# One of nine harmonics taken out of the product on TensorE, and harmonics loaded in longer runs

## The reference

```python
def tensor_product(x_e, sh, w, C):            # C: [64, 9, 128]
    acc = sh[:, 0:1] * (x_e @ C[:, 0, :])
    for s in range(1, S):                     # S = 9 harmonics
        acc = acc + sh[:, s:s + 1] * (x_e @ C[:, s, :])
    return acc * w
q = (tfn_features @ Wq).reshape(n, H, DQK)
k = tensor_product(x_dst, edge_sh, wk, Cqk).reshape(-1, H, DQK)
v = tensor_product(x_dst, edge_sh, wv, Cv).reshape(-1, H, DV)
attn = jnp.einsum('ehd,ehd->eh', q[edge_src], k)
...                                           # softmax over the edges of a node, sum of v * alpha,
out = tfn_features @ W_self + upd             # W_out, then a batch norm
```

## Time and profile before

| | |
|---|---|
| median of 3 runs | 3127.47 us (3126.22 to 3128.46) |
| profiled execution, span from first to last instruction | 3126.1 us |
| what lies around the span (median less span) | 1.4 us |
| busy over the whole span | PE 79%, PEld 68%, DVE 71%, ACT 28%, POOL 65% |

### The profile page before, as it was taken

The page is one execution under the profiler, slowest core; times in us unless marked ns, Lnnn a source line. Parts: engine busy times, 40 slices in busy tenths (PEclk is TensorE's granted clock), DMA queues, the critical chain, the costliest instruction groups (busy, mean ns, idle before and its releaser), DMA issues. The chain is left out here.

```text
span 3126.1 us, 51454 instructions
## 1 busy us (share of the span) xinstructions
PE 2476.7 (79%) x14006; PEld 2130.6 (68%) x14006; DVE 2209.2 (71%) x5060; ACT 864.2 (28%) x2414; POOL 2032.3 (65%) x2119
## 2 busy tenths in 40 slices
PE   5778787525667667477777767999999999999986
PEld 4777787424666666355555556888888888888862
DVE  4555555526888887555555563888888888888875
ACT  1111111136666663111111110222232222323231
POOL 4777777457777771277777736777776677677710
PEclk9776667657888888599999978999999999999985
DMA  3443333133333330155555557889888898888820
GB/s 84 94 89 86 86 87 86 30 68 64 61 60 60 60 52 4 46 155 160 152 160 152 160 147 179 214 206 214 212 206 205 203 216 206 207 204 205 213 68 11
DMA packets 333760, 404.38 MB, mean 129 GB/s; under 512 B 171136, under 2 KB 203006, under 8 KB 333570
## 3 DMA queue, kind: packets, MB, share of 16 engines
q1 hardware_dynamic: 252034, 251.20, 34.4%
q0 software_dynamic: 66560, 96.41, 14.5%
q10 hardware_dynamic: 14976, 54.53, 5.1%
HBM read 339.81 MB, written 62.07 MB: 129 GB/s over the span
## 5 line engine op out<-in xcount | busy, mean ns | idle before, releaser
L1934 PE MATMUL psum<-ckv,z 128*128 128x256 f32 x4160 | 967.8, 383 | 0.0
L1934 PEld LDWEIGHTS psum<-ckv,z 128*128 128x128 f32 x4160 | 766.7, 191 | 97.9
L1768 POOL DMA_INDIRECT acc<-QW,dst_i x416 | 399.5, 960 | 184.6 <-issue 111.2
L234 POOL DMA_INDIRECT ga<-TA,src_i x416 | 412.4, 991 | 161.6 <-issue 126.5
L1789 POOL DMA_INDIRECT ga<-XX,src_i x416 | 399.5, 960 | 162.8 <-issue 122.5
L1027 POOL DMA_INDIRECT ga<-T,src_i x416 | 401.9, 966 | 151.5 <-issue 125.9
L234 POOL DMA_INDIRECT ga<-T,src_i x416 | 396.6, 953 | 149.3 <-issue 124.7
L2048 DVE TENSOR_TENSOR z<-psum,shb 128x2560 f32<-128x2560 f32 x104 | 293.2, 2820 | 66.7 <-PE psum L1925 66.5
L1121 PE MATMUL psum<-HT,wy 128*128 128x128 f32 x1664 | 264.7, 324 | 70.0 <-DVE wy L1394 69.2
L445 PE MATMUL psum<-wre,re 128*128 128x68 f32 x832 | 215.2, 351 | 119.4 <-DVE oneT L290 67.7
L1121 PEld LDWEIGHTS psum<-HT,wy 128*128 128x128 f32 x1664 | 242.8, 232 | 87.8 <-DVE wy L1394 81.5
(11 more groups left out here) (362 smaller groups left out, 4142.9 us busy)
## 6 DMA issues: line engine op xcount, KB each, us to landing
shb<-in_ea SPq DMA_DIRECT2D x104, 640.0 KB, 6.2
WKV<-wkvo ACTq DMA_DIRECT2D x104, 512.0 KB
shb<-in_ea SPq DMA_DIRECT2D x104, 512.0 KB, 8.5
wkv<-WKV SPq DMA_DIRECT2D x104, 512.0 KB
dl<-DL SPq DMA_DIRECT2D x208, 128.0 KB
win<-TB SPq DMA_DIRECT2D x416, 32.0 KB
ga<-T,src_i POOLq DMA_INDIRECT x832
ef<-in_ea SPq DMA_DIRECT2D x104, 128.0 KB
```

Source lines behind the costliest of these rows:

```text
L234: pool.indirect_dma_start(o, None, table, bass.IndirectOffsetOnAxis(ap=src_i[:, g * GT + t:g * GT + t + 1], axis=0)).then_inc(s_g[k], 16)
L1768: pool.indirect_dma_start(qg[:, (g % QR) * GT + t, :], None, QW, bass.IndirectOffsetOnAxis(ap=dst_i[:, g * GT + t:g * GT + t + 1], axis=0) ...
L1934: last = pe.matmul(kv_of(k)[:, t, :], z[:, k % 2, j, t * 128:(t + 1) * 128], ckv[:, j, :], start=(j == 0), stop=(j == NZ - 1))
```

## The change

The ninth harmonic leaves the product on PE. Its keys and values without the harmonic, `h @ C[:, 8, :]`, are computed once per node (`node_last_harmonic`), copied by DVE to SBUF and written as 256 more columns of `XX`, whose rows are now 384 columns (1536 bytes) instead of 128 (512 bytes). After the gather ACT multiplies those 256 columns of each edge by its ninth harmonic, a scale per partition, and writes the result into PSUM (`last_harmonic`); PE adds the remaining four chunks onto it without clearing it. `seen` runs four matmuls into those banks ahead of the stage. DVE's `z` has four chunks (2048 elements). The ring of gathered rows has three groups instead of four. The host lays out the harmonics so that each partition's run in a load is 8 KB, and the ninth as a column per tile. The node queries are moved behind the new node products. `h` is written to `XX` from `H` by two transfers a half, in 256-byte pieces, and ACT's copy into `twice` is gone.

```diff
-        NZ = 5
+        NZ = 4
+        TR3 = 2 * D + 2 * F
-        XX = dram("XX", [N, 2 * D])
+        XX = dram("XX", [N, TR3])
-        GR = 4
+        GR = 3
...
                     if g >= GR:
                         pool.wait_ge(e3_X, g - GR + 1)
+                        pool.wait_ge(e3_seed, g - GR + 1)
...
-                    sp.dma_start(shb[0:D, k % 2], A["ea9"][0:NS:2, cols].partition_broadcast(D)).then_inc(e3_e[k % 2], 16)
-                    sp.dma_start(shb[D:128, k % 2, 0:NZ - 1], A["ea9"][1:NS:2, cols].partition_broadcast(D)).then_inc(e3_e[k % 2], 16)
+                    sp.dma_start(shb[0:D, k % 2].rearrange("p z e -> p (z e)"),
+                                 A["sh_even"][g:g + 1, :].partition_broadcast(D)).then_inc(e3_e[k % 2], 16)
+                    sp.dma_start(shb[D:128, k % 2].rearrange("p z e -> p (z e)"),
+                                 A["sh_odd"][g:g + 1, :].partition_broadcast(D)).then_inc(e3_e[k % 2], 16)
...
-                    sp.wait_ge(n3_x, h + 1)
-                    sp.dma_start(XX.rearrange("(p j) f -> p j f", p=PN)[:, J, :], twice[:, J].rearrange("p j a f -> p j (a f)")).then_inc(n3_ox, 16)
+                    sp.wait_ge(n3_h, h + 1)
+                    for a in range(2):
+                        sp.dma_start(XX.rearrange("(p j) f -> p j f", p=PN)[:, J, a * D:a * D + D], H[:, J, :]).then_inc(n3_ox, 16)
+                for part in PARTS:
+                    sp.wait_ge(n3_bc, pairs(part[1]))
+                    sp.dma_start(XX.rearrange("(p j) f -> p j f", p=PN)[:, J_of(part), 2 * D:TR3], parts_of[:, J_of(part), :]).then_inc(n3_ox, 16)
...
+                def last_harmonic(i, k):
+                    g = i * UG + k
+                    act.wait_ge(e3_g[k], i * 64 + 64)
+                    wait(act, e3_ev, (g - 1) * 2)
+                    for t in range(GT):
+                        last = act.activation(kv_of(k)[:, t, :], ga[:, (i * UG + k) % GR * GT + t, 2 * D:TR3], ACT.Copy,
+                                              scale=sh_last[:, bass.ds(g * GT + t, 1)])
+                    last.then_inc(e3_seed, 1)
...
                 def products(i, k, t):
                     g = i * UG + k
                     if t == 0:
                         pe.wait_ge(e3_z, g + 1)
-                        wait(pe, e3_ev, (g - 1) * 2)
+                        pe.wait_ge(e3_seed, g + 1)
                     for j in range(NZ):
                         last = pe.matmul(kv_of(k)[:, t, :], z[:, k % 2, j, t * 128:(t + 1) * 128], ckv[:, j, :],
-                                         start=(j == 0), stop=(j == NZ - 1))
+                                         start=False, stop=(j == NZ - 1), skip_group_check=True)
...
+                def node_last_harmonic(r):
+                    j0, n = R3[r]
+                    pe.wait_ge(n3_tc, r + 1)
+                    if r >= 2:
+                        pe.wait_ge(n3_bc, pairs(r - 1))
+                    for j in range(n):
+                        last = pe.matmul(bank[4 + r % 2 * 2 + j // 2][0:PN, j % 2 * 256:j % 2 * 256 + 256],
+                                         HT[:, (j0 + j) * PN:(j0 + j + 1) * PN], c_last[:], start=True, stop=True)
+                        if j % 2 or j == n - 1:
+                            last.then_inc(n3_b, 1)
...
+                for r, (j0, n) in enumerate(R3):
+                    for half, (a, m) in enumerate(rounds(n, 2)):
+                        dve.wait_ge(n3_b, pairs(r) + half + 1)
+                        dve.tensor_copy(parts_of[:, j0 + a:j0 + a + m, :],
+                                        bank[4 + r % 2 * 2 + half][0:PN, 0:m * 256].rearrange("p (j f) -> p j f", j=m)).then_inc(n3_bc, 1)
```

More of the change, by code:

```diff
@@ L1708, in build @@
         NODE3 = len(R3) * 5 + 2
+        pairs = lambda r: sum(len(rounds(n, 2)) for _, n in R3[:r])
+        NOX = 2 * len(HALVES) + len(PARTS)
         e3_zero = sem("e3_zero")
@@ L1720, in build @@
         SPARE = 8
-        ga = tmp("ga3", [128, GR * GT, F])
-        one = tmp("one3", [128, OR * GT, 128])
+        rows3 = tmp("rows3", [128, GR * GT * TR3 + OR * GT * 128])
+        ga = rows3[:, 0:GR * GT * TR3].rearrange("p (t f) -> p t f", f=TR3)
+        one = rows3[:, GR * GT * TR3:GR * GT * TR3 + OR * GT * 128].rearrange("p (t n) -> p t n", n=128)
+        parts_of = rows3[0:PN, 0:NJ * 2 * F].rearrange("p (j f) -> p j f", j=NJ)
         wkv = tmp("wkv", [128, 2, GT, 2 * F])
@@ L1896, in _ @@
                     act.activation(HT[0:D, j0 * PN:(j0 + n) * PN], bank[r % 2][0:D, 0:n * PN], ACT.Copy).then_inc(n3_tc, 1)
-                    if r:
-                        query_rows(r - 1)
-                query_rows(len(R3) - 1)
+                for r in range(len(R3)):
+                    query_rows(r)
                 act.wait_ge(e3_i, 3)
+                act.wait_ge(n3_ox, NOX * 16)
+                act.wait_ge(n3_l, NL3 * 16)
+                act.wait_ge(n3_seen, 4)
                 each_step(act, body)
@@ L1924, in transposes @@
                     for t in range(GT):
[L1925 removed]
+                        last = pe.transpose(bank[0][:, t * 128:(t + 1) * 128], ga[:, (i * UG + k) % GR * GT + t, 0:2 * D], ident[:])
                     last.then_inc(e3_X, 1)
@@ L1970, in node_transposes, with seen @@
                     for j in range(n):
-                        last = pe.transpose(bank[r % 2][0:D, j * PN:(j + 1) * PN], twice[:, j0 + j, 0, :], ident[0:PN, 0:PN])
+                        last = pe.transpose(bank[r % 2][0:D, j * PN:(j + 1) * PN], H[:, j0 + j, :], ident[0:PN, 0:PN])
                     last.then_inc(n3_t, 1)
+                def node_last_harmonic(r):
[8 more added lines that the diff above has]
+                            last.then_inc(n3_b, 1)
+                def seen():
+                    for b in range(2, 6):
+                        pe.matmul(bank[b][:], ident[:], ckv[:, 0:2, :].rearrange("p a f -> p (a f)"), start=True, stop=True)\
+                          .then_inc(n3_seen, 1)
                 def node_queries(r):
@@ L1994, in _ @@
                     if r:
-                        node_queries(r - 1)
-                node_queries(len(R3) - 1)
+                        node_last_harmonic(r - 1)
+                node_last_harmonic(len(R3) - 1)
+                for r in range(len(R3)):
+                    node_queries(r)
                 pe.wait_ge(n3_qc, len(R3))
-                pe.wait_ge(n3_p, 4)
+                pe.wait_ge(n3_bc, pairs(len(R3)))
+                pe.wait_ge(n3_p, 3)
+                seen()
                 pe.sem_inc(e3_S, SPARE)
@@ L2030, in _ @@
                 for J, _ in HALVES:
-                    dve.scalar_tensor_tensor(twice[:, J, 0, :], XC[:, J, :], 0.0, st[:, 5, J].unsqueeze(2).to_broadcast([PN, J.stop - J.start, D]),
+                    dve.scalar_tensor_tensor(H[:, J, :], XC[:, J, :], 0.0, st[:, 5, J].unsqueeze(2).to_broadcast([PN, J.stop - J.start, D]),
                                              ALU.max, ALU.mult).then_inc(n3_h, 1)
@@ L2251 @@
     a["ea64"] = np.pad(a.pop("edge_attr_64"), ((0, fill), (0, 0))).T
-    a["ea9"] = np.pad(a.pop("edge_attr_9"), ((0, fill), (0, 0))).T
+    ea9 = np.pad(a.pop("edge_attr_9"), ((0, fill), (0, 0)))
+    a["sh_last"] = ea9[:, 8].reshape(NT, W).T
+    ea9 = ea9.reshape(NT // GT, GT * W, 9).transpose(0, 2, 1)
+    a["sh_even"] = ea9[:, 0:8:2].reshape(NT // GT, -1)
+    a["sh_odd"] = ea9[:, 1:8:2].reshape(NT // GT, -1)
     a["L2_gnn_WT"] = a.pop("L2_gnn_W").T
```

31 lines of the change are left out of this document (15 added, 16 removed).

## The result

The changed kernel takes 3166.20 us (median of 4 runs, 3143.56 to 3186.18) against 3127.22 before: ratio 1.012, 95% interval 1.0089 to 1.015. It is 1.2% slower, where 3100 was forecast. Its four runs lie 43 us apart, those of the kernel before 2 us. The profiled execution took 3162.97 us with a span of 3161.2, 35.1 more than before.

A forecast was written before the change was run, and what follows sets the result against it. PE was taken as the bound at 10.76 us a group; 10.1 after the change gives -67 us in the stage, +42 ahead, -2 at the end: -27, so 3100 us, range 3072 to 3131.

The forecast's parts named there:

- What bounds the kernel before: Fourth edge stage: PE is the bound at 10.76 us a group, with DVE 0.3 and POOL 0.8 us behind.
- PE's gain, DVE's, z: Per group: PE loses 8 of 40 instructions, 1.86 us, leaving 8.9; DVE's z shrinks by 0.56 us, leaving DVE 9.9.
- ACT's four instructions "at nothing": Scaling after the gather: 1.4 to 2.9 us of ACT a group, costed at nothing; without cover up to 0.7 a group.
- The ring "nothing": Gathered rows in the stage: three groups instead of four leave 17 us of slack, so no cost.
- The harmonics at the old rate: Harmonics loads in the stage: 8 KB runs bring nothing, the rate stays, q1 takes 6.8 us a group.
- The inventory of the DMA: Stage, all 16 engines per group: q1 6.8 us, XX gathers 2.6 to 3.1, QW 1.0, sum 10.4 to 10.9.
- With 1.07 as full, 9.7 to 10.2 us: Stage: dividing the DMA work by a full share of 1.07 gives 9.7 to 10.2 us a group, as near binding as DVE.
- POOL's 10.0 us: Stage: eight gathers a group at 0.95 us work plus 0.30 between make 10.0 us, POOL becoming the bound.
- rival 4: Stage gathers: POOL's issue grows with the row; each 0.1 us costs 42 us, at 0.15 3163 us; chance 0.07.
- The shift ahead of the stage: Table writes before the first gather: longer writes start the stage 42 us later, bounds 24 and 46.
- Rival 2: XX writes from H: 256-byte writes cost far more than loads; at three times 22 ns, 3155 us; chance 0.13.
- Rival 1: Stage: DMA by bytes, softmax steps or ACT's queue hold a group at 10.35 us; 3126, no change; chance 0.16.

The follow-up runs named there:

- before_light: The kernel before, with its harmonics loads bringing only five of the nine harmonics from the third group on: 3127.94 us, ratio 0.9998.
- no_seed: The changed kernel without ACT's four scalings a group, so the ninth harmonic is missing from the sums, all gathered as before: 3168.58 us, ratio 1.0134.
- light_loads: The changed kernel with the harmonics loads bringing only 4 KB of each partition's 8 KB from the third group on: 3111.52 us, ratio 0.9947.
- ring4: The changed kernel with the ring of gathered rows back at four groups: 3166.26 us, ratio 1.0121.
- before_long_runs: The kernel before with only the change's DRAM layout of the harmonics, one run of 10 or 8 KB into each partition: 3127.85 us, ratio 0.9999.
- two_queues: The changed kernel with the odd harmonics' loads issued by ACT two groups ahead, the even ones still by SP: 3208.00 us, ratio 1.0247.
- light_values: light_loads with DVE's product of values and weights cut to one column in sixteen from the third group on: 3088.59 us, ratio 0.9872.
- single_h: The changed kernel with rows of 320 columns (h once), eight PE products by the identity replacing four transposes, and a four-group ring: 3115.74 us, ratio 0.9969.
- distinct_source: The changed kernel with each partition's 8 KB of harmonics loaded from a DRAM row of its own: 3141.82 us, ratio 1.0061.

## Why the prediction was wrong

The order of its steps:

- **What bounds the kernel before** was right: PE, shown by before_light.
- **PE's gain, DVE's, z** were right in size: 32 instructions of products a group, z 2.287 us for 2.27 forecast. PE's clock stayed near full (0.96).
- **ACT's four instructions "at nothing"** was right: no_seed gains nothing. In no_seed the DMA still holds the stage, so it alone would not show this; but in light_loads, where the DMA does not, PE never waits for ScalarE either. They took 4 x 0.463 = 1.9 us, inside 1.4 to 2.9.
- **The ring "nothing"** was right in the sum (ring4). The sign I had named for being wrong, GpSimd waiting on its shorter ring, did appear (44.7 us), but as an effect of late rows.
- **The harmonics at the old rate** was right within the 5% that before_long_runs found. Alone they load at 216 GB/s (212 before). Distinct rows in DRAM leave q1 as it was. The half of the ports that the Trainium skill gives (SBUF — State Buffer, "Door 1: the DMA port swizzle") is neither refuted nor shown; two_queues shows that issuing the loads of both halves at once gains nothing.
- **The inventory of the DMA** was right: 6.69 us for q1 (6.8 forecast) and 3.79 for both gathers (3.6 to 4.1), 10.5 in all (10.4 to 10.9).
- **"With 1.07 as full, 9.7 to 10.2 us" is the step that failed.** I took the share of 9 us in which one kind of load ran with nothing else as the capacity of a stage in which two kinds of gathers and three of loads mix and each load waits for its buffer. In the changed kernel the same 9 us read 1.00 (first row below), and the six kernels that are held by the DMA show 0.97 to 1.01 over 900 us; why a mixed stretch ends there is not shown. 10.5 / 0.97 is 10.8 us, and the rest of the chain followed: PE, VectorE and GpSimd each wait in turn for rows that are late. Of the miss in the stage, 101 x 0.76 = 77 us, light_loads gives 101 x (10.86 - 10.37) = 49 to it.
- **POOL's 10.0 us was mis-sized too**: it is 10.37, the other 0.27 us of the miss against the 10.1 I took, 27 us in all. A gather's price was read as 0.95 us at the stage's start and 0.96 in the steady part; where GpSimd itself is the bound the mean is 0.98 to 1.00, since products of two SBUF tiles hold gathers up. One such product costs 0.21 us a group (light_values against light_loads). The row's length costs nothing (rival 4 falls). The kernel before paid less of this because fewer of its gathers met such a product: between 2000 and 2900 us 29 of 678 were held, against 105 of 695 in light_loads. That it was GpSimd's waiting for VectorE which kept them apart is argued, not shown.
- **The shift ahead of the stage** was +26 to +31, not +42, within the bounds of 24 and 46. Packets of 256 bytes took 0.399 x 12 x 16 / 4256 = 18 ns, of 1,024 bytes 0.34 x 20 x 16 / 2370 = 46 ns, where 22 and 50 were forecast; and shares of 0.40 and 0.34 are 6.4 and 5.4 engines, not five. Rival 2, dear writes below 512 bytes, falls: 18 ns is no more than loads of that size cost (20.4 ns at 221 bytes), so nothing of the read-modify-write for which I had cited the Trainium skill (DMA: Bandwidth & Descriptors, "Specifications") shows in the price. By the byte they are still 1.6 times as dear as the packets of 1,024.

The harmonics' loads alone, 1850 to 1859 us, and the queue's rows for the two stretches of writes, 1864 to 1876 and 1883 to 1903 us:

```profile
1850.00:1859.00 9.00, 2.85 (x10) 2.48 (x10) 8.28 (x25) 1.25 (x3) 0.00 (x0) 0.50 1.00 216
...
q1 hardware_dynamic: 4256, 1.09, 39.9%
...
q1 hardware_dynamic: 2370, 2.42, 34.0%
```

Put right, the sum is 101 x (10.86 - 10.76) + 26 - 1 = +35 us. The sum would have been near it with the same inventory and 0.97: 10.8 us a group, +4 in the stage. Rival 1 named the mechanism (DMA by bytes) but stopped at 10.35 us; with DMA bytes taken away the stage does stop there, at 10.37, and the change would then have gained 0.5%, as light_loads did.

## What to carry to other kernels

When PE is the bound and the next resources lie within 5 to 10%, moving PE's work into gathered rows pays with the resource that has no idle engine to show for it: add up the DMA's time for a group and hold it against the share that a long mixed stretch reaches, 0.97 to 1.01 here, not against a peak of a few microseconds. Take the price of an instruction from the stretch where its neighbours run, not from the stage's first ones. And a duplicated column in a gathered row is paid on every gather; PE could make the copy (single_h), which, with the ring of four, turned a loss of 1.2% into a gain of 0.3%.

## What the runs showed of the hardware

- A gather issued by GpSimd that begins while VectorE works on two SBUF tiles is held and ends 0.81 to 0.83 us after that product (105 gathers of light_loads): up to 1.46 us in place of 0.94. Products of PSUM and SBUF do not hold it: beside `z` gathers take 0.94 to 0.96. A copy of 0.22 us costs one 0.03 us (light_loads). The product itself takes 0.69 us with or without a gather under way.
- The same bytes cost the DMA engines 10.2 us a group (distinct_source), 10.5 (the changed kernel) and 11.2 (two_queues). The gathers differ most: 3.6, 3.8 and 4.3 us. A full share is not the reason, since the same gathers take 3.9 us at a share of 0.72 (light_loads).
- Issuing the loads of the two halves of the partitions on two queues was slower (11.13 us a group for 10.86).
